# One more wait on GpSimd: each gather of the expert stage waits for TensorE's first signal

## What is computed

```python
x = _layernorm(x + attention(x))
xt = x.reshape(-1, D)                                # 8192 tokens
w, idx = jax.lax.top_k(jax.nn.softmax(xt @ Wg.T), 2)
w = w / (w.sum(axis=-1, keepdims=True) + 1e-20)
cw = zeros((T, E)).at[arange(T)[:, None], idx].add(w)
h = silu(einsum('td,ehd->teh', xt, W1)) * einsum('td,ehd->teh', xt, W3)
y = einsum('te,ted->td', cw, einsum('teh,edh->ted', h, W2))
x = _layernorm(x + y)
```

## Time and profile before

| | us |
|---|---|
| median of 3 runs | 982.62 |
| the 3 runs | 981.38, 983.60, 982.62 |
| the profiled execution, its own time | 989.87 |
| its span, first to last instruction | 988.1 |
| expert stage in it: first gather issued | 500.29 |
| first scatter issued | 525.63 |
| last gather issued | 917.89 |
| last scatter issued | 940.19 |

### The profile page before, as it was taken

How to read it: one execution, slowest core, us unless ns; L and a number is a source line. 1 busy time by engine, 2 the same in 40 slices (tenths; PEclk the granted TensorE clock), 3 DMA queues, 4 the chain that set the end, 5 groups by cost and what they waited for, 6 DMA issues and landing times. The chain is left out here.

```text
span 988.1 us, 22538 instructions
## 1 busy us (share of the span) xinstructions
PE 799.6 (81%) x7657; PEld 598.8 (61%) x7658; DVE 585.2 (59%) x1478; ACT 480.5 (49%) x1150; POOL 552.4 (56%) x719
## 2 busy tenths in 40 slices
PE   5899999999999999982538877888777778787866
PEld 3556666666666666551228776877767777686722
DVE  4678888888888888827935433434434343343445
ACT  1377777777777777755713222222223222222347
POOL 6146666666666666654054666656665656666543
PEclk9899999999999999975668988898998898999979
DMA  5334444434434443204921111111111111112178
GB/s 168 103 122 134 135 135 134 132 131 129 127 127 136 135 135 129 75 8 176 163 46 30 44 41 44 41 41 42 44 43 39 43 42 43 43 42 43 36 238 280
DMA packets 71596, 93.98 MB, mean 95 GB/s; under 512 B 10336, under 2 KB 50016, under 8 KB 71232
## 3 DMA queue, kind: packets, MB, share of 16 engines
q1 hardware_dynamic: 62640, 74.21, 24.1%
q0 software_dynamic: 8704, 17.98, 7.0%
q10 hardware_dynamic: 144, 0.35, 0.1%
HBM read 56.26 MB, written 34.14 MB: 91 GB/s over the span
## 5 line engine op out<-in xcount | busy, mean ns | idle before, releaser
L377 DVE TENSOR_REDUCE neg_max<-ps_s 128x6 f32<-128x768 f32 x256 | 241.1, 952 | 38.7 <-PE ps_s L564 32.7
L242 POOL TENSOR_SCALAR_AFFINE_SELECT probs<-probs 128x512 f32<-128x512 f32 x256 | 162.4, 634 | 164.7 <-ACT probs L314 159.1
L314 ACT ACTIVATE probs<-ps_st 128x768 f32<-128x768 f32 x256 | 207.5, 811 | 81.5 <-PE ps_st L578 80.9
L1122 ACT ACTIVATE act_a<-ps_a 128x352 f32<-128x352 f32 x136 | 63.5, 467 | 310.7 <-DMA dense<-shift_t 160.4
L1103 POOL DMA_INDIRECT picked_rows<-rows_out,pairs x136 | 134.0, 986 | 134.1 <-ACT rows_out L1126 109.9
L1096 POOL DMA_INDIRECT xg<-x_rows,pairs x136 | 131.6, 968 | 79.8 <-issue 40.5
L1160 DVE TENSOR_TENSOR x_low<-ps_xy,x_high 128x128 fp32r<-128x128 f32 x136 | 39.1, 287 | 216.6 <-ACT x_high L1130 173.6
L558 PE MATMUL ps_s<-dense 32*128 32x256 f32 (+1 forms) x1024 | 117.9, 306 | 19.1 <-ACT probs L314 9.3
L1231 PE MATMUL ps_xy<-w_sb,h_t 128*128 (+1 forms) x816 | 129.2, 300 | 1.7 <-ACT rows_out L1126 1.7
L558 PEld LDWEIGHTS ps_s<-dense 32*128 32x128 f32 x1024 | 82.2, 191 | 78.2 <-issue 46.7
L1231 PEld LDWEIGHTS ps_xy<-w_sb,h_t 128*128 128x128 f32 (+1 forms) x816 | 120.6, 213 | 7.1 <-issue 6.8
(11 more groups left out here) (181 smaller groups left out, 1390.6 us busy)
## 6 DMA issues: line engine op xcount, KB each, us to landing
dense_rows<-split SPq DMA_DIRECT2D x32, 512.0 KB, 2.7
dense<-dense_rows SPq DMA_DIRECT2D x64, 256.0 KB
dense<-dense_rows SPq DMA_DIRECT2D x64, 128.0 KB
pick<-picked_rows SPq DMA_DIRECT2D x16, 512.0 KB, 6.0
x_rows<-y_all SPq DMA_DIRECT2D x8, 520.0 KB, 8.1
xt_sb<-xt SPq DMA_DIRECT2D x32, 128.0 KB, 2.2
x_sb<-x SPq DMA_DIRECT2D x32, 128.0 KB, 2.4
out<-normal SPq DMA_DIRECT2D x16, 256.0 KB
```

The source lines that it names most:

```text
L242: last = pool.affine_select(out=part, in_=part, compare_op=ALU.is_ge, fill=0.0, base=0, pattern=[[0, 2 * BLOCKS], [1, P]], channel_multipl ...
L314: act.activation(probs[:, g, 2 * half:2 * half + 2, 0:L + P], ps_st[:, :, 0:L + P], ACT.Exp, scale=float(HEAD_DIM) ** -0.5).then_inc(exp_d ...
L377: v.tensor_reduce(out=neg_max[:, h * GROUP + j:h * GROUP + j + 2, :], in_=ps_s[:, j:j + 2, 0:L + P].rearrange("p b (c t) -> p b c t", t=P) ...
```

## The change

Ahead of each gather GpSimd now waits for TensorE's first signal of one iteration:

```diff
@@ in the loop of GpSimd
             for s in range(n + LEAD):
                 if s < n:
                     wait(pool, share_ready, s - ROWS_IN)
+                    front(pool, s - LEAD + BEHIND)
                     pool.indirect_dma_start(
                         out=xg[:, s % ROWS_IN, :], out_offset=None, in_=x1_rows,
```

## The result

The changed kernel takes 970.36 us (median of four runs, 968.96 to 1021.86), the kernel before beside it 983.01 us (981.38 to 983.60). The ratio is 0.9874, with a 95% interval of 0.9852 to 0.9896: 12.4 us less, 1.3%. (The run of 1021.86 us was disturbed, at a granted clock of 0.737, and stays out of the ratio.) The direction of the forecast is right, its size is not: 950 us were forecast, with 930 to 968 us as the forecast's own range.

What follows compares the result with a forecast made beforehand. No engine is full: GpSimd's work holds TensorE's signals, then GpSimd idles waiting for `rows_out`. Idle time -32, start -3, wait instruction +2 give -33 us, from 982.6 to 950 us; own range 930 to 968, 8-in-10 range 915 to 1000.

Steps and rivals of the forecast that it cites:

- The mechanism: Expert stage: TensorE's signals reach ScalarE late (held) while GpSimd works and come through 1.10 to 1.34 us after it stops.
- a transfer that lands: Named as what would make the forecast wrong: a landing transfer, not GpSimd's pause, lets a held signal through; no chance given.
- Where it is idle: Steady part: idle time moves from scatter to gather, 1.2 us instead of 1.82, 51 times: 32 us less.
- The wait instruction: Ahead of each gather: a met wait costs nothing visible, an extra instruction 0 to 6 us over 123 gathers; 2 us taken.
- Who stands behind it: On GpSimd only the same step's scatter stands behind the wait; the gathered tile's lateness costs nothing.
- where GpSimd lags behind: In the middle of a GpSimd run the signal is already there; order and times stay, 2.56 us a pair.
- The start: First 13 gathers: GpSimd idles earlier, so the held signal could come sooner; 3 us gained, ends 0 and 5.
- A VectorE copy that shuts GpSimd out: Copy of `h` beside gathers: taken as 0; if the skill's rule applied, up to 68 us, near 1018 us; 2 in 100.
- Held after every pair: Rival, slower: TensorE and GpSimd in lockstep, 3.46 us a tile, 34 us more, about 1015 us; chance 23 in 100.
- the 0.69: Share f of held tiles at which 2.56 + 0.9 f equals 3.18 us a tile; it was 0.41 before.
- Not GpSimd's doing: Rival, no change: signals late for TensorE's own reason, idle time only moves; 983 us, 978 to 987; chance 17 in 100.
- No signal held any more: Rival, much faster: the pause ahead of each gather suffices, GpSimd's 2.56 us pairs bound; 904 us, up to 925; 8 in 100.

Runs made afterwards that it cites:

- the third group: Kernel before, 988.57 us; change, 976.11; the waits swapped, 965.26; kernel before with SyncE plain copies for GpSimd's gathers, 854.3, on a place with held signals.
- the waits swapped: Changed kernel with the gather's two waits reordered, front_done before share_ready, so the gather carries the signal's wait: 956.97 us, ratio 0.9735; again 965.26 us, ratio 0.9775.
- the start alone: Changed kernel with the new wait only ahead of the first 13 gathers, steady part as in the kernel before: 977.53 us, ratio 0.9957.
- the first traces: Profiled executions of changed kernel against kernel before: steady part 378.6 us where it took 391.0, start 20.1 us where it took 26.6.
- the steady part alone: Changed kernel with the new wait only from the 14th gather on, start burst as in the kernel before: 976.72 us, ratio 0.9945.

## Why the prediction was wrong in size

**The mechanism** has two halves. That signals are held while GpSimd works without a break is borne out: the semaphores' own records show it, and in the third group nothing is held once GpSimd's gathers are gone. That GpSimd's pause releases them is not shown. The release at 1.16 and 1.17 us after GpSimd's end lies in the forecast's 1.10 to 1.34 us, but 9 of 49 releases before the change fall into GpSimd's next instruction. The forecast named the rival itself, a transfer that lands. For it: 24 of the 49 releases before and 35 of the 47 after lie within 0.1 us of a recorded landing of a gather or scatter (582.22 beside 582.21 us), where some 20 in 100 would by chance. Against it: with the waits swapped only 7 of 61 do, and in 49 the landing comes 0.1 to 0.3 us behind the release. So what lets a signal through stays open.

**Where it is idle: the step that failed.** The idle time of 1.82 us was to become 1.2 us, 51 times, -32 us. Measured: 1.94 us, 40 times, -12.3 us in the traces. The step took the time from GpSimd's last instruction to ScalarE's Silu for the time to GpSimd's own next instruction, and put the gather's delay behind the signal at nothing. Both see the signal at once, but the gather starts 0.72 us later where the wait is an instruction of its own, and 0.23 us later where the gather carries it. The steady part missed the forecast by 378.6 - 359 = 20 us. With the waits swapped, which brings the idle time to the forecast's 1.2 us, it takes 368.2 us. So 10.5 us, half of the miss, goes with the length of the idle time, two thirds of which (0.49 of 0.75 us) is that delay and one third the earlier release. The other half, 9.2 us, is a second error in the same term: it kept the number of idle times fixed. The number held in neither kernel: 40 with the change and 62 with the waits swapped, where 51 were taken. With shorter idle times GpSimd is further into its run when the next signal is due, and in the swapped kernel, of the first signals due over 2 us into a run, 101 of 103 come late.

**The wait instruction:** costed at 0 to 6 us, all in the case that the wait is already met. That holds: 0.30 us between instructions throughout. The case that costs, a wait that is not met, was costed at nothing.

**Who stands behind it, and where GpSimd lags behind:** right. Scatters wait 4.5 us in all, pairs stay at 2.56 us.

**The start:** 3 us taken, with 0 to 5 as ends; 4.6 us by the runs of the start alone, 6.6 us in the first traces and 5.3 us in those of the third group. The step was right, its size a little small: the first scatter is issued at 518.19 us, not 525.63.

**A VectorE copy that shuts GpSimd out:** not seen. Gathers take 968 ns and scatters 988 ns with the change too. The rule of the Trainium skill (SBUF — State Buffer, section Who interferes with whom) did not apply to these copies out of PSUM.

**The rivals.** *Held after every pair:* not seen with the change, 43 waits and not over 85. With the waits swapped the shares go that way (62 of 123, 0.50) and stay under the 0.69 from which it costs. *Not GpSimd's doing:* falls with the third group. The idle times after the change look like it (1.94 us, where 1.81 were before), but for another reason. By the Trainium skill (Perfetto Trace Analysis, section Tensor Engine Instruction) a matmul's end is worked out and its signal comes later; here, on a place without held signals, the Silu starts 0.03 us after that end, so the 3.5 and 4.8 us of the cycle are no such lag. *No signal held any more:* the forecast had it as what the change might do. It is what some places do by themselves, 898 to 900 us, and the change has no part in it.

**The forecast's sum, again:** -32 should have been -5 (the runs of the steady part alone), with -12 by the first traces and -3 by those of the third group; -3 some -5; +2 nothing. Its base was right: the median took off the 7 us by which the profiled execution was too long.

**A version that beats both** is the swapped order: 956.97 and 965.26 us where the kernel before takes 982 and 987. It was not run on a place without held signals; as the wait there is always met, no difference is to be expected, but this is only argued.

**What stays open:** what decides whether a place holds signals (two groups with the same recorded chip number gave 898 and 987 us); what lets a held signal through, and why it comes 0.25 us sooner with the waits swapped; whether it is the descriptor writing or the transfers that hold it; whether GpSimd's other work does it too; whether its gathers alone do.

## What to carry to other kernels

When an idle time is to be moved from one instruction to another, take the new one's own delay from signal to start as a price, and see which of its waits the instruction carries itself: the wait that is met last should be that one. When a stall comes back in a circle, ask for the number of stalls as well as for their length; shorter stalls that came more often were worth a third of what their length alone would have saved here (10.5 of 30 us). And if a kernel's time differs by 9% between places, find out first which stall is behind it, since what mends that stall is worth nothing on the other places.

## What the runs showed of the hardware

- **TensorE's semaphore signals can arrive microseconds late while GpSimd issues indirect DMAs back to back**, and only TensorE's: ScalarE's and VectorE's came within 0.02 us of their instructions' ends in the same traces. In the changed kernel 71 of 73 first signals that were due over 3 us into a run of GpSimd's came more than 0.1 us late, and 4 of 34 under 2 us into one. Most of the held ones come through 0.9 to 1.3 us after the end of an instruction of GpSimd's (32 of 49 before and 37 of 47 after, with GpSimd idle).
- **It depends on the place.** In three of the six groups of runs the kernel before took 982 to 987 us, and the traces taken there with its gathers on GpSimd show held signals. In the other three it took 898 to 900 us, and no trace from them shows one: in the changed kernel there, all 125 first signals due over 3 us into a run came within 0.02 us.
- **A wait in an instruction of its own on GpSimd, not yet met, delays the indirect DMA behind it by 0.5 us**: it starts 0.72 us after the signal instead of 0.23. Swapping the two waits, which takes that delay away and brings the signal through 0.25 us sooner, was worth 11 to 13 us in 960 (970.36 to 956.97, 976.11 to 965.26).
- **Indirect DMAs of 128 rows on GpSimd** took 0.97 to 0.99 us with 0.30 us between them in the steady part, before and after the change, and two of them for a tile, 2.56 us, bound this kernel where signals were not held.
